# Expert outputs of 16 units as seven half-size products, woven into the next unit; PSUM banks by first release

## What is computed

```python
k = int(EXPERT_CAPACITY * t / e)                       # 2 * 512 / 8 = 128 tokens per expert and batch
g, m = jax.lax.top_k(probs.transpose(0, 2, 1), k)
xin = x[batch_idx, m]                                  # gathered rows, 128 x 256
h = jnp.einsum('nekd,edf->nekf', xin, w1)              # 256 -> 1024
h = jax.nn.gelu(h, approximate=False)
h = jnp.einsum('nekf,efd->nekd', h, w2)                # 1024 -> 256, the second product
out = zeros.at[batch_idx, m].add(g[..., None] * h)     # then x + gb * out
```

## Time and profile before

| | us |
|---|---|
| median of 3 runs | 1877.31 (1876.67 to 1879.22) |
| the profiled execution, its own time | 1877.36 |
| its span, first to last instruction | 1876.1 |
| PE busy / DVE busy / ACT busy / POOL busy | 1853.5 / 1186.1 / 933.5 / 725.4 |
| units 12 to 27 (starts of their `index` products) | 1587.51 to 1813.02 |
| units 28 to 31 to the end of the span | 1813.02 to 1876.1 |

### The profile page before, as it was taken

One profiled execution on the slowest core, in us unless ns is written; L12 is line 12 of the kernel. 1 busy time (PEld: TensorE's weight loads), 2 busy tenths in 40 slices (PEclk: granted clock), 3 DMA queues, 4 the chain that ended last, 5 costly groups with the idle time before them and its releaser, 6 DMA issues.

```text
span 1876.1 us, 32761 instructions
## 1 busy us (share of the span) xinstructions
PE 1853.5 (99%) x12217; PEld 1301.1 (69%) x12217; DVE 1186.1 (63%) x3064; ACT 933.5 (50%) x1968; POOL 725.4 (39%) x803
## 2 busy tenths in 40 slices
PE   8999999999999999999999999999999999999998
PEld 5656566756665676666566655666787898999997
DVE  7677675567466665856675464577765679556641
ACT  4657665565556555655655575455344332222221
POOL 3213344324333533343244334344453444535432
PEclk9999999999999999999999999999999999999999
DMA  4200010001000100000010000040121243233334
GB/s 134 80 26 1 12 39 3 23 1 41 1 23 1 40 22 3 26 16 24 1 40 13 1 12 15 25 137 1 38 76 28 50 107 89 43 82 85 82 83 115
DMA packets 59724, 76.95 MB, mean 41 GB/s; under 512 B 7128, under 2 KB 52848, under 8 KB 59312
## 3 DMA queue, kind: packets, MB, share of 16 engines
q1 hardware_dynamic: 46464, 57.28, 9.2%
q0 software_dynamic: 12288, 16.79, 5.3%
q10 hardware_dynamic: 816, 0.79, 0.1%
HBM read 53.71 MB, written 21.00 MB: 40 GB/s over the span
## 4 chain that ended last, share of the span: by engine, by line
PE 95%; DVE 2%; ACT 1%; issue 1%; DMA 0%; POOL 0%; SPq 0%; ACTq 0%; POOLq 0%; DVEq 0%
PE bank L815 15%; PE bank L1096 11%; PE bank L884 8%; PE bank L1052 5%; PE bank L939 4%; PE bank L908 4%; PE bank L832 4%; PE bank L920 4%; PE bank L1046 4%; PE bank L952 3%; PE bank L893 3%; PE bank L800 3%; PE bank L634 3%; PE bank L870 2%; PE bank L762 2%; PE bank L665 2%
## 5 line engine op out<-in xcount | busy, mean ns | idle before, releaser
L1947 POOL TENSOR_TENSOR s<-s,ri 128x256 f32<-128x256 f32 (+3 forms) x128 | 159.7, 1260 | 202.5 <-DVE ri L1672 202.5
L1096 PE MATMUL bank<-ew,h 128*128 128x256 f32 x1024 | 227.4, 379 | 0.0
L1096 PEld LDWEIGHTS bank<-ew,h 128*128 128x128 f32 x1024 | 192.2, 190 | 26.0 <-issue 1.2
L1997 POOL DMA_INDIRECT out<-y,indices x64 | 102.5, 1602 | 240.9 <-DVE y L1834 140.6
L1650 DVE SCALAR_TENSOR_TENSOR th<-th,bank 128x384 f32<-128x384 f32 (+1 forms) x192 | 104.0, 593 | 133.2 <-ACT th L1305 133.2
L1314 ACT ACTIVATE s<-s,mn 128x128 f32<-128x128 f32 (+3 forms) x256 | 140.8, 551 | 84.9 <-DVE mn L1665 83.7
L1679 DVE COPY pT<-bank 128x384 f32<-128x384 f32 (+1 forms) x192 | 106.0, 593 | 91.6 <-PE bank L920 91.6
L884 PE MATMUL bank<-look,term 128*128 128x384 f32 (+3 forms) x512 | 152.8, 437 | 0.0
L815 PE MATMUL bank<-hT,wqkv 128*128 128x512 f32 x320 | 149.3, 601 | 0.0
L815 PE MATMUL bank<-hT1b,wqkv 128*128 128x512 f32 x320 | 148.4, 600 | 0.3 <-ACT hT1b L1167 0.3
L1910 POOL TENSOR_SCALAR look<-look 128x768 f32<-128x768 f32 (+1 forms) x96 | 87.8, 914 | 154.6 <-ACT look L1286 153.8
(11 more groups left out here) (353 smaller groups left out, 4081.3 us busy)
## 6 DMA issues: line engine op xcount, KB each, us to landing
ew<-L_ffn_w SPq DMA_DIRECT2D x24, 1024.0 KB, 7.9
x1s<-x_scratch SPq DMA_DIRECT2D x8, 512.0 KB, 5.8
out<-x1s SPq DMA_DIRECT2D x8, 512.0 KB, 2.9
xn_scratch<-n_xn SPq DMA_DIRECT2D x8, 512.0 KB, 2.9
x<-L_attn_x SPq DMA_DIRECT2D x7, 512.0 KB, 3.8
x_scratch<-x SPq DMA_DIRECT2D x7, 512.0 KB, 3.0
wqkv<-w_qkv SPq DMA_DIRECT2D x1, 3072.0 KB, 10.0
wqkv<-L_wmod SPq DMA_DIRECT2D x2, 1024.0 KB, 7.0
```

The costliest lines, as they stand in the source:

```text
L1096: mm = te.matmul(banks[i][:, 0:D], ex.h1[:, g, half * P:(half + 1) * P], w2[:, g, :], start=(g == 0), stop=(g == FC - 1))
L1947: done = g.tensor_tensor(sc, sc, b1.ri[u % 2][:, m, :].unsqueeze(2).to_broadcast([P, 2, w]), ALU.mult)
L1997: g.indirect_dma_start(out=k.d["out"], out_offset=bass.IndirectOffsetOnAxis(ap=ex.index[:, b, half:half + 1], axis=0), in_=ex.y[w % 3][:, ...
```

## The change

1. **Second product of units 12 to 27** (`ends_in_seven`: experts from 4 on). Step `output` is replaced by four steps `ends` 0 to 3: seven half-size products, each of four matmuls with 128 columns, into three banks. ScalarE copies three parts out, VectorE adds them, and gate and `gb` are multiplied in SBUF. The sums of the hidden values (`mix_h_first`, `mix_h`) are four VectorE operations on 128 x 512 floats per unit. The sums of `w2` are four more GpSimd additions for each of the four experts, put in step `seven` 2 of the unit before the expert.
2. **Weaving.** `ends` i of unit m-1 stands behind `seven` i (or `hidden` i) of unit m, so that `h1` has two buffers. `mix_x(b)` moves from the end of the unit before to `seven` 0, behind the sums of the last unit's tail; `turn_x` stands behind `seven` 1 (or `hidden` 1). The load of the weights behind an expert is issued when its last `ends` is done.
3. **Banks.** Each product takes the bank whose release stands first in the list; the fifth and the second product of `seven` share one bank.
4. **Order.** All three tables are written anew, with the same steps. In `HEAD` the load of `x` goes ahead of the first modulation weights, and the filler transposes stand at other places, as many as before.

The new buffers lie over `wqkv1` and `vc1`, which are dead by then. The core of the diff (the tables, `h1` as `ex.h1[buffer_of(b)]` and declarations are left out):

```diff
+ENDS_FROM = 4
+def ends_in_seven(m):
+    return seven(m) and UNITS[m][2] >= ENDS_FROM
...
+    first = "seven" if seven(m) else "hidden"
+    woven = m > 0 and ends_in_seven(m - 1)
+    for i in range(4):
+        yield first, m, i
+        if woven and i == 1 and m + 1 < NUNIT:
+            yield "turn_x", m + 1, 0
+        if woven:
+            yield "ends", m - 1, i
+        if i == 0 and m + 3 < NUNIT:
             yield "pick", m + 3, 0
+        if i == (2 if seven(m) else 1) and not woven and m + 1 < NUNIT:
+            yield "turn_x", m + 1, 0
...
+    if woven and m - 1 == LAST_OF[n] and n + NBUF < E + FIRST:
         yield "weights", n + NBUF, 0
+    if not ends_in_seven(m):
+        for i in range(2):
+            yield "output", m, i
...
+def released(step, b, n, i):
+    if step == "su":
+        return "sw", b, n
+    if step == "seven" and n < 2:
+        return step, b, 3 - n
+    if step == "ends" and n == 0:
+        return step, b, 2 + i
+    return step, b, n
...
-            bank = banks[turn % len(banks)]
+            bank = min(free, key=free.get)
+            free[bank] = position[released(step, b, n, i)], turn
...
 TensorE
+        elif step == "ends":
+            def summed(bank, rows, cols, first, last):
+                for g in range(FC // 2):
+                    mm = te.matmul(banks[bank][:, 0:P], rows(g), cols(g), start=first and g == 0, ...)
+            if n == 0:
+                te.wait_ge(s["mixed_h"], 4 * nth_ends + 1)
+                te.wait_ge(s["mixed_ends"], 4 * (load - ENDS_FROM + 1))
+                te.wait_ge(drained[iz], nz - 1)
+                summed(iz, h1s[0], w2[right])
+                te.wait_ge(s["sevened"], 3 * b + 3)
+                te.wait_ge(drained[ix], nx - 1)
+                summed(ix, h1[left], w2[left])
+            elif n == 1:
+                te.wait_ge(drained[iy], ny - 1)
+                summed(iy, ...)
+                te.wait_ge(s["mixed_h"], 4 * nth_ends + 3)
+                te.wait_ge(s["tail_copied"], 3 * nth_ends + 2)
+                summed(ix, ...)
+            elif n == 2:
+                te.wait_ge(s["mixed_h"], 4 * nth_ends + 4)
+                summed(iz, ...)
+                te.wait_ge(s["tail_copied"], 3 * nth_ends + 3)
+                summed(ix, ...)
+            else:
+                te.wait_ge(s["tail_read"], nth_ends + 1)
+                summed(ix, ...)
...
 ScalarE
+        elif step == "ends" and n < 2:
+                a.copy(ex.part[:, 0, :], banks[iz][:, 0:P])
+                a.copy(ex.part[:, 1, :], banks[ix][:, 0:P])
+                a.copy(ex.part[:, 2, :], banks[ix][:, 0:P])
...
 VectorE
+    def mix_h_first(m):
+        v.wait_ge(s["sevened"], 3 * m + 2)
+        v.tensor_tensor(h1s[:, 0, :, :], h1[:, tops, right], h1[:, lows, right], ALU.add)
+    def mix_h(m):
+        v.wait_ge(s["sevened"], 3 * m + 3)
+        v.tensor_tensor(h1s[:, 2, :, :], h1[:, tops, left], h1[:, tops, right], ALU.subtract)
+        v.tensor_tensor(h1s[:, 1, :, :], h1s[:, 0, :, :], h1[:, tops, left], ALU.subtract)
+        v.tensor_tensor(h1s[:, 3, :, :], h1[:, lows, left], h1s[:, 1, :, :], ALU.subtract)
...
+            if n == 0 and b > 0 and ends_in_seven(b - 1):
+                mix_x(b)
+                mix_h(b - 1)
...
+            elif n == 3:
                 v.wait_ge(full[i1], n1)
+                if ends_in_seven(b):
+                    mix_h_first(b)
+                if seven(b + 1) and not ends_in_seven(b):
+                    mix_x(b + 1)
...
+        elif step == "ends":
+            if n == 1:
+                v.tensor_tensor(y[:, 0:P], banks[iy][:, 0:P], ex.part[:, 1, :], ALU.add)
+            elif n == 2:
+                v.tensor_tensor(first[:, P:2 * P], banks[iz][:, 0:P], ex.part[:, 2, :], ALU.add)
+                v.scalar_tensor_tensor(out=first[:, :], in0=first[:, :], scalar=gate, in1=gb, ...)   # y_done
+                v.tensor_tensor(y[:, P:2 * P], banks[ix][:, 0:P], ex.part[:, 0, :], ALU.add)        # tail_read
+            elif n == 3:
+                v.tensor_copy(y[:, 0:P], banks[ix][:, 0:P])
+                v.scalar_tensor_tensor(out=y[:, :], in0=y[:, :], scalar=gate, in1=gb, ...)            # y_done
...
 GpSimd
+        elif step == "seven" and n == 2 and new_ends(b + 1):
+            g.wait_ge(k.weights_in[load % NBUF], 32 * (load // NBUF + 1))
+            g.tensor_tensor(sums[:, 1, :, :], w2[:, lower, right], w2[:, upper, right], ALU.subtract)
+            g.tensor_tensor(w2[:, upper, right], w2[:, upper, right], w2[:, upper, left], ALU.subtract)
+            g.tensor_tensor(sums[:, 0, :, :], w2[:, lower, right], w2[:, upper, right], ALU.subtract)
+            g.tensor_tensor(sums[:, 2, :, :], w2[:, lower, left], sums[:, 0, :, :], ALU.subtract)
+        elif step == "ends" and n >= 2:
+            g.wait_ge(s["y_done"], 2 * k.nth_ends[b] + half + 1)
+            g.wait_ge(s["added"], 16 * w)
+            g.indirect_dma_start(out=k.d["out"], ..., in_=ex.y[w % 3][:, :], compute_op=ALU.add)
```

More of the change, by code:

```diff
@@ L58 @@
[L58 to L67, removed]
@@ L141 @@
+    choice1 experts choice1 experts*2 choice1 choice1 choice1 experts*3 choice1 experts*2
 """
@@ L204, in new_load @@
     return seven(m) and UNITS[m][2] != UNITS[m - 1][2]
+FIRST_ENDS = min(m for m in range(NUNIT) if ends_in_seven(m))
 def experts_steps(m):
@@ L276, in products @@
         return SEVEN[n]
+    if step == "ends":
+        return ENDS[n]
     return PRODUCTS.get(step, 0)
+def released(step, b, n, i):
[6 more added lines that the diff above has]
+    return step, b, n
 def psum_places(order):
     at, had = {}, [0] * 8
-    turn = -1
-    banks = (0, 1, 3, 4, 5, 6, 7)
+    position = {step: x for x, step in enumerate(order)}
+    free = {bank: (-1, x) for x, bank in enumerate((0, 1, 3, 4, 5, 6, 7))}
+    turn = len(free)
     for step, b, n in order:
         for i in range(products(step, b, n)):
+            bank = min(free, key=free.get)
+            free[bank] = position[released(step, b, n, i)], turn
             turn += 1
-            bank = banks[turn % len(banks)]
             had[bank] += 1
@@ L463, with __init__ @@
 class Experts:
-    def __init__(self, sb):
+    def __init__(self, sb, over, over_vc):
         self.w1 = [sb(f"ew1{i}", [P, KC, F]) for i in range(NBUF)]
         self.w1s = [sb(f"ew1s{i}", [P, 3, F // 2]) for i in range(NBUF)]
+        self.w2s = [over(f"ew2s{i}", [P, 3, FC // 2, P]) for i in range(NBUF)]
+        self.h1s = over("h1s", [P, 4, FC // 2, P])
+        self.part = over("part", [P, 3, P])
         self.w2 = [sb(f"ew2{i}", [P, FC, D]) for i in range(NBUF)]
@@ L525, in __init__ @@
         self.at = psum_places(self.order)
+        self.nth_ends = {m: i for i, m in enumerate(m for m in range(NUNIT) if ends_in_seven(m))}
         self.sem = {n: nc.alloc_semaphore(n) for n in SEMAPHORES}
@@ L549, in __init__ @@
                     for layer in range(2)]
-        self.ex = Experts(Arena(nc, middle, end))
+        self.ex = Experts(Arena(nc, middle, end), Arena(nc, self.b1.wqkv_at, self.b1.wqkv_end),
+                          Arena(nc, self.b1.vc_at, self.b1.vc_end))
+        self.last_of_wqkv = [x for x in self.order if x[0] in ("proj", "vc")][-1]
 N_POOL_CONST = 15
@@ L1064, in tensor_engine @@
                 te.wait_ge(s["mixed_x"], 4 * (b + 1))
-                te.wait_ge(drained[i5], n5 - 1)
-                product(i5, sums[:, 0, :], xt[:, 0, :]).then_inc(full[i5], 1)
+                te.wait_ge(drained[i2], n2 - 1)
+                product(i2, sums[:, 0, :], xt[:, 0, :]).then_inc(s["fifth"], 1)
                 te.wait_ge(s["first_read"], b + 1)
@@ L2112, in sync_engine @@
             if b >= NBUF:
-                i, nth = at["output", LAST_OF[b - NBUF], 1, 0]
+                last = LAST_OF[b - NBUF]
+                i, nth = at["ends", last, 0, 1] if ends_in_seven(last) else at["output", last, 1, 0]
                 sp.wait_ge(full[i], nth)
```

318 lines of the change are left out of this document (205 added, 113 removed).

## The result

| | before | after |
|---|---|---|
| median of 6 runs | 1877.09 us (1876.67 to 1879.22) | 1885.26 us (1883.56 to 1886.50) |
| ratio after / before | | 1.0041, 95% interval 1.0031 to 1.0051 |
| span of the profiled execution | 1876.1 us | 1884.5 us |
| busy: TensorE, VectorE, GpSimd | 1853.5, 1186.1, 725.4 us | 1847.7, 1251.8, 756.2 us |
| TensorE's mean granted clock | 1.000 | 0.995 |

A forecast was written before the change was run, and what follows sets the result against it. The prediction took TensorE, busy 1853.5 of 1876.1 us at full clock, as the bound. Terms of -13.1 + 9.6 + 1.5 + 1.0 - 4.0 = -5.0 gave 1872.4 from 1877.36, stated as 1872.3 us, range 1858 to 1886.

The forecast's parts named there:

- columns and weaving: Units 12 to 28: narrower second product and fewer eviction waits make a woven unit 13.25 us, 13.1 us gained.
- exclusion, three experts: the wait: Before experts 5 to 7: GpSimd's additions shut out VectorE, `mix_x` comes late, TensorE stalls 3.2 us each, 9.6 us lost.
- expert 4 in unit 11, and units 12 and 13 behind it: waits: Unit 11: four new GpSimd additions meet the top-k's last steps, 1.5 us lost (0 to 3).
- load for unit 29: waits: Before unit 29: weights issued after unit 27's tail land late, a stall of 1 us (0.8 to 1.2).
- banks and order: Products outside the experts: 39 fewer short bank reuses at 0.1 us, 4 us gained; order from 10 us gained to 7 lost.
- VectorE's load: Ordinary woven units: VectorE needs 12.1 of 13.25 us, costs nothing, with a cover of some 0.4 us.
- signs that the prediction named for being wrong: Ordinary units above 13.7 us, unit 12 starting over 10 us from 1583.5, or no idle at the three boundaries.
- the exclusion eats the gain: Rival at the first units of experts 5 to 7: 6.5 us lost each, 19.5 in all, 1883.7 us; chance 0.17.
- turning point of 5 us per expert: Loss per expert at experts 5 to 7 from which the forecast sum passes zero.
- the tables give nothing: Rival: all terms as forecast but the banks' 4 us, 1876.3 us, no change; chance 0.15.
- exclusion in full: Range's upper end: the slow rival at experts 5 to 7, plus 2 us lost by the tables, 1886 us; chance 0.17.

The follow-up runs named there:

- filler: Kernel after with 24 filler transposes on TensorE ahead of the product waiting for `mix_x`, in the first units of experts 5 to 7: 1880.76 us.
- early_split_filler: `early_split` plus 20 filler transposes on TensorE ahead of the wait for the ranks before `index` of unit 12: 1866.32 us, 0.9948 of before.
- sums_thin: Kernel after with GpSimd's additions on `w2` cut to one column in 128, TensorE reading `w2` itself (result not right): 1870.18 us, 0.9962 of before.
- sums_early: Kernel after with GpSimd's four additions on `w2` one unit earlier for all experts: 1877.11 us, 0.9997 of before.
- sums_late: Kernel after with GpSimd's four additions on `w2` one unit later, in the expert's own first unit, for all four experts: 1879.87 us, 1.0013 of before.
- banks_only: Kernel before, its own tables and units, with only the new bank rule: 1878.18 us, 1.0001 of before.
- tables_banks: Kernel after with no unit in the new form, only new tables, list and bank rule: 1876.54 us, 0.9993 of before.
- split: Kernel after with separate semaphores for the two weight loads, `w1` issued after its last first product, `w2` as before: 1880.68 us, 1.0016 of before.
- early_split: Kernel after with additions on `w2` one unit earlier for experts 5 to 7 only, plus the edit of `split`: 1868.00 us, 0.9946 of before.
- late_split: Kernel after with the edits of `sums_late` and `split` together: 1877.70 us, 1.0002 of before.

## Why the prediction was wrong

Term by term, against the bookkeeping above:

| term | forecast | measured | difference |
|---|---|---|---|
| columns and weaving | -13.1 | -13.63 | -0.5 |
| exclusion, three experts: the wait | +9.6 | +9.1 (3 x 3.02) | -0.5 |
| expert 4 in unit 11, and units 12 and 13 behind it: waits | +1.5 | +3.0 | +1.5 |
| load for unit 29: waits | +1.0 | +2.8 | +1.8 |
| banks and order | -4.0 | -0.75 | +3.2 |
| TensorE at 1.2 GHz behind five idle times | none | +8.0 | +8.0 |
| sum | -5.0 | +8.4 | +13.4 |

(Rounded to 0.1; the parts add up to 8.4 before rounding.) The 8.0 us are 4.7 of the three stalls (17.82 - 16.25, three times), 1.56 of unit 12, and for unit 29 1.7, half of 3.4 us; the first are isolated by a run of their own (`filler`), the second is seen from the other side in `early_split_filler` and in unit 12 of `sums_thin` (7.19 us), the third against `sums_early` and `sums_late` (1.6 us).

**Columns, weaving, VectorE's load: right.** A woven unit lasts 13.23 us, forecast 13.25, and the groups start 0.89 us apart. In an ordinary unit VectorE keeps up and costs nothing, as forecast, though its busy time rose by 65.7 us over the kernel.

**The exclusion: right, in mechanism and in size.** Forecast: eight additions within 11 to 12 us, VectorE's additions at 1.3 us and more beside them, TensorE idle 2 to 4 us three times. Found: eight additions in 1643.82 - 1632.65 = 11.2 us, 1.35 and 1.23 us, idle 2.77. The prediction put `mix_x` between 18 us (let in behind each addition) and 20.4 us (only at gaps) after the start of the unit before; it ended at 1643.97 - 1624.94 = 19.0. The prediction's "one row shows the hold over two additions, the others are silent" misread the trace of before: the two VectorE rows behind the earlier trace rows show the other case, one operation in the gap at 0.28 us and one held for a single addition.

```profile
1696.11 0.28 DVE L1392 TENSOR_TENSOR xint<-xin 128x128 f32<-128x128 f32 x1
1696.31 1.35 DVE L1394 TENSOR_TENSOR xint<-xin,xint 128x128 f32<-128x128 f32 x1
```

After the change `mix_x` goes this way too. The rule that the prediction took from the Trainium skill's page SBUF — State Buffer ("Who interferes with whom"), that the one engine blocks for the whole instruction of the other, holds here: 1.35 us beside 1.26 us.

**What a stall costs: the step that failed.** The sentence "a stall of 4.2 us ... a stall of 1.8 ... I take the middle, 3.2 us" prices a stall at its idle time. I had noted that the clock "is granted in full in every slice", though its digits of 9 only say 90% or more in 47 us, and drew from it only that TensorE is the bound, not that there was a clock to lose. Each microsecond figure of the exclusion, of expert 4 and of the load lacked the 1.6 us behind it. With this one term and all the rest as it stood, the sum would have been +3.0: on the slow side, though within 0.2%. In the trace of before the largest idle time in this stretch was the earlier trace rows's 1.33 us, after which the clock stayed; that the same place can lose it is seen only in `banks_only`. None of the signs that the prediction named for being wrong came: the three boundaries show their idle time, ordinary units last 13.23 us and unit 12 starts 5.5 us from 1583.5. None of them looked at the clock.

**Banks and order: wrong.** The step was 39 fewer short reuses times the 0.1 us of the earlier trace rows. Two runs show 0.9993 and 1.0001, and both intervals hold 1. The 0.1 us stood between two blocks with different operands; nothing showed it to be the price of a bank, and it was multiplied 39 times. That is the second largest error, 3.25 us.

**Expert 4: too low.** Forecast 1.5 (0 to 3); unit 11 lost 2.27 (2.6 against the 16.16 of `tables_banks`), and `index` waited 2.56 us, long enough for the clock to fall. That unit 12 starts "some 4 us earlier" failed with it: it starts 1.5 later, 1589.03. The 0.72 us of unit 13 do not come from these additions, since its wait of 0.59 us at the first product stands in `sums_thin` too; the prediction had no term for the short unit 12.

**The load: the place was right, the size wasn't.** 2.24 us of idle time instead of 1.0. The median of 24 loads stood for the one that mattered, which took longer.

**The rivals.** The slow one, "the exclusion eats the gain", had the time (1883.7) and the wrong reason: the following units do not pay on, they last 13.23 us, and its 6.5 us per expert were 4.6. Its turning point of 5 us per expert wasn't reached; the sum passed zero because four other terms were off to the same side. The rival "the tables give nothing" held in its mechanism, by both runs.

**Slips in the recorded sums.** The middle of stalls of 1.8 and 4.2 us is 3.0 us, not 3.2; measured were 3.0. The rival without the tables' gain and with the columns at 0.93 comes to 1876.3 + 6.1 = 1882.4, not "about 1878". The upper end of the range, "exclusion in full and 2 us lost by the tables", is 1877.3 + 10.4 + 2 = 1889.7, not 1886. Two thirds of 0.40 are 0.27, not 0.29. None of them changes the side of the forecast.

## What to carry to other kernels

In a kernel whose bounding engine runs at full clock without a break, price a stall of 1.5 us or more as its idle time plus some 1.6 us for the slow stretch behind it, which came in 14 of the 17 stalls of 1.5 to 2.8 us in these traces, and look for the clock in a window of a few microseconds, since a page in 40 slices hides it. When an addition on GpSimd is to be hidden, look not for idle time on GpSimd but for a stretch in which no operation of VectorE with both inputs in SBUF stands on the path, and look at the first and the shortest round of the pipeline by themselves: three placements here were right for the ordinary units and two of them were undone in units 11 to 13. A difference of 0.1 us between two rows with different operands is no price to multiply.

## What the runs showed of the hardware

- **TensorE's clock falls behind short idle times, but not behind each.** In the traces of all twelve kernels, from 60 to 1860 us, 17 idle times of TensorE lie between 1.5 and 2.8 us. Eleven of them were followed by 3.4 us at the 1.2 GHz level instead of the 2.4 GHz level, the shortest being 1.52 us (`banks_only`), at a price of some 1.6 us where it could be read by itself; three, all ahead of unit 12 (`filler`, `split`, `early_split`), by 6.8 us at a price of 2.6; and three of 2.56 to 2.77 us (`sums_late`, `sums_early`, `split`) by none. One of 1.33 us (before) was followed by none either.
- **Beside longer idle times the slow stretch lies in part in the idle time itself**, where it costs nothing: 5.57, 8.1 and 9.49 us of idle time came with 6.8, 10.2 and 13.6 us at half clock (`sums_early`, `late_split`, `sums_late`), which began before the idle time had ended.
- Every stretch at half clock in this part of the traces goes with one of these idle times. The Trainium skill's page TensorE: Matmul & The Clock Gate (Part 1) ties the fall from 2.4 to 1.2 GHz to idle time of the engine; the traces agree with that.
- **Work that computes nothing holds the clock.** 24 transposes in the wait saved 1.6 us of each 4.6 (`filler`).
- **VectorE can be held through two GpSimd additions back to back**: 3.08 us for an operation of 0.28 (`sums_early`), though in after `mix_x` was let in at each gap. What decides was not settled.
- **A cast seems to be held as well.** In one row each, the CAST of 128 x 2 elements with one input takes 0.98 us beside the additions (L1906 above) and 0.17 us without them, in `early_split`:

```profile
1640.41 0.17 DVE L1908 CAST indices<-token 128x2 uint32<-128x2 f32 x1
1640.49 0.28 DVE L1496 TENSOR_TENSOR xint<-xin 128x128 f32<-128x128 f32 x1
```
